# A router gate, state tables and the hand-written order of all steps rewritten in a two-layer kernel

## The reference

```python
xn = layernorm(x)                                    # layer 0
s  = complex_recurrence(xn; 32 states, A, B, C) + D * xn
g  = silu(gelu(xn @ proj1.T + b1) @ proj2.T + b2)    # hidden 1024
x  = x + s * g
xn = layernorm(x)                                    # layer 1
s  = causal_attention(xn; 16 heads, latent kv of 64, rope of 64) @ Wo
logits = xn @ router_w.T + router_b                  # 8 experts
p  = softmax(logits); keep the two largest, divide by their sum -> gate
g  = silu(xn @ base_w.T + base_b + 2 * ((xn @ lora_A) * gate) @ lora_B)
x  = x + s * g
```

## Time and profile before

| | us |
|---|---|
| median of 3 runs | 942.93 |
| lowest and highest | 942.03, 947.07 |
| the profiled execution, its own time | 945.76 |
| its span, first to last instruction | 944.0 |
| mean granted TensorE clock | 0.965 |
| busy: PE, PEld, DVE | 852.4, 770.8, 739.1 |
| busy: ACT, POOL | 544.0, 478.7 |

### The profile page before, as it was taken

The page is one execution under the profiler, slowest core; times in us unless marked ns, Lnnn a source line. Parts: engine busy times, 40 slices in busy tenths (PEclk is TensorE's granted clock), DMA queues, the critical chain, the costliest instruction groups (busy, mean ns, idle before and its releaser), DMA issues.

```text
span 944.0 us, 22803 instructions
## 1 busy us (share of the span) xinstructions
PE 852.4 (90%) x7632; PEld 770.8 (82%) x7632; DVE 739.1 (78%) x2611; ACT 544.0 (58%) x1612; POOL 478.7 (51%) x1188
## 2 busy tenths in 40 slices
PE   5778999999898589999999998999999899899986
PEld 4567998888787579798898987989889797897974
DVE  6798878988587378888888877788877888868872
ACT  4433444444545556667566675666766576665671
POOL 5722101201315466666666666576766666656661
PEclk9989999999999799999999999999999999999997
DMA  8401110000001111111111111111111111111110
GB/s 309 158 1 29 57 56 1 1 1 1 2 12 42 37 37 46 37 48 32 47 46 39 48 29 48 34 49 47 32 49 34 48 45 32 51 28 46 47 31 13
DMA packets 56278, 41.22 MB, mean 44 GB/s; under 512 B 30304, under 2 KB 53216, under 8 KB 55520
## 3 DMA queue, kind: packets, MB, share of 16 engines
q1 hardware_dynamic: 56160, 39.75, 15.3%
HBM read 14.53 MB, written 4.19 MB: 20 GB/s over the span
## 4 chain that ended last, share of the span: by engine, by line
PE 54%; DVE 23%; SPq 11%; issue 6%; POOL 4%; DMA 1%; ACT 1%; POOLq 0%; DVEq 0%; ACTq 0%
PE bank L454 32%; PE bank L640 10%; PE bank L658 7%; SPq L408 5%; SPq L420 5%; DVE SM L1424 5%; DVE PT L1444 4%; DVE qa L1411 2%; POOL par L1616 2%; POOL par L1621 1%; PE bank L516 1%; DVE st L1304 1%; PE bank L606 1%; DMA QT<-qa 1%; DVE xn L1271 1%
## 5 line engine op out<-in xcount | busy, mean ns | idle before, releaser
L1739 POOL TENSOR_SCALAR SM<-SM,stb 128x256 f32<-128x256 f32 (+1 forms) x512 | 212.2, 431 | 137.3 <-DVE stb L1432 134.7
L907 ACT ACTIVATE SM<-SM,stb 128x256 f32<-128x256 f32 (+1 forms) x512 | 226.5, 444 | 61.9 <-DVE stb L1424 60.9
L640 PE MATMUL bank<-KT,QT 128*128 128x256 f32 (+1 forms) x1024 | 206.4, 341 | 45.0 <-DVE stb L1424 33.4
L640 PEld LDWEIGHTS bank<-KT,QT 128*128 128x128 f32 x1024 | 155.1, 195 | 68.3 <-DVE stb L1424 40.1
L1424 DVE CUSTOM_DVE_ANT_0 SM<-bank,CONST 128x256 f32<-128x256 f32 (+1 forms) x512 | 155.3, 349 | 15.7 <-PE bank L640 14.3
L1444 DVE STREAM_TRANSPOSE PT<-SM 128x512 f32<-128x512 f32 x192 | 135.1, 704 | 39.2 <-PE bank L658 36.9
L454 PE MATMUL bank<-yh,wq_lo 128*128 128x256 f32 x512 | 157.2, 307 | 0.0
L454 PE MATMUL bank<-yh,wq_hi 128*128 128x256 f32 x512 | 144.3, 282 | 0.0
L454 PE MATMUL bank<-yl,wq_hi 128*128 128x256 f32 x512 | 144.2, 282 | 0.0
L795 ACT ACTIVATE hs<-bank,B 128x512 f32<-128x512 f32 x64 | 44.1, 689 | 94.5 <-PE bank L454 76.9
L454 PEld LDWEIGHTS bank<-yh,wq_lo 128*128 128x128 f32 x512 | 96.7, 189 | 1.6
(11 more groups left out here) (185 smaller groups left out, 2105.9 us busy)
## 6 DMA issues: line engine op xcount, KB each, us to landing
QT<-qa SPq DMA_DIRECT2D x512, 32.0 KB, 1.9
C<-KV SPq DMA_DIRECT2D x256, 16.0 KB, 1.8
out<-fo SPq DMA_DIRECT2D x32, 128.0 KB, 1.8
X<-in_x SPq DMA_DIRECT2D x7, 512.0 KB, 10.4
stage<-in_wqn SPq DMA_DIRECT2D x2, 1024.0 KB, 5.1
stage<-in_wo SPq DMA_DIRECT2D x2, 1024.0 KB, 5.1
stage<-in_w1t SPq DMA_DIRECT2D x4, 256.0 KB, 4.5
stage<-in_w2t SPq DMA_DIRECT2D x2, 512.0 KB, 5.6
```

What stands on the lines that cost most here:

```text
L640: i = e.matmul(sbank[n % 2][:, nk * j:nk * j + nk], Q[:, h % 8, 128 * qt:128 * qt + 128], KT[b % 3][:, h % 2, 0:nk], start=True, stop=True)
L907: i = e.activation(M[:, nk * j:nk * j + nk], M[:, nk * j:nk * j + nk], ACT.Exp, bias=S[:, 0, j:j + 1], scale=-1.0, accum_out=S[:, 1, j:j + 1])
L1739: i = e.tensor_scalar(P[:, nk * j:nk * j + nk], P[:, nk * j:nk * j + nk], S[:, 2, j:j + 1], 1.0, ALU.mult, ALU.mult)
```

## The change

It does the following.

- Gate: `e.max` gives the eight largest in order for each token tile; the third to eighth are overwritten with 3e38, `e.match_replace` puts -1e30 where the first two are found, in the logits and in a field of 3e38 at once, and one subtraction each gives two arguments for exp, whose difference is the gate. ACT's exp takes 32 columns for 16. POOL fills one field instead of the ramp (1 memset for 8). `GATE_REST` is 10 for 9.
- Tables: cosine and sine lie side by side, so one instruction does both products and sums of a doubling step (3 for 4), and the copies at the end are 5 for 10. One more piece boundary.
- POOL's parameters: the exponentials of both columns of `nuth` are made in one pass, so three passes become two; the eight multiples of the angle are issued with no wait in between. The load of `nuth` goes ahead of those of x.
- First chunks: `scan(0)` at g=9 (7), `scan(1)` and later at 12, 20, ... as before; `l0_bu(0)` at 6 (7); the outputs of chunk 1 a step later; the tables start at g=6 (3); `l0_sum` and `l0_gate` a step later for all chunks.
- Last batch: `l1_pv`, `latents` and `latents_low` for tile 0 come as soon as its units are turned (step 12 after the batch's start instead of 16), and its `l1_out` at 15 instead of 19; tile 1 follows alone.
- Passage: all eight query blocks of batch 0, and all four placements in the order 0, 3, 1, 2, come ahead of the first step; before, three placements came ahead and the fourth at step 4, behind `spread(0)`. `gate_sum(0)` comes after the four `turn_queries`.
- Other steps: `Q_AT`, `TK_AT`, `MISC_AT`, the bank order and the place of nearly every call in its step. In a batch `l1_lora` now comes first in step 9, ahead of the query block, the misc block and the turn of the keys; `mids` comes a step later on ACT; `gate_sum` comes ahead of `most`; `weigh` a step earlier.

```diff
-Q_AT = {0: (0,), 2: (1,), 5: (2, 3), 9: (5,), 10: (7, 6), 11: (4,)}
-Q0_AT = {2: (5,)}
+Q_AT = {1: (0,), 2: (1,), 5: (2, 3), 9: (7,), 10: (5,), 11: (6, 4)}
+Q0_AT = {}
-TURN_AT, TM_AT, TK_AT, LORA_AT, MISC_AT = 7, 7, 8, 9, (8, 11)
-GATE_REST = 9
+TURN_AT, TM_AT, TK_AT, LORA_AT, MISC_AT = 7, 7, 9, 9, (9, 10)
+GATE_REST = 10
...
-def summed(n, lag):
+def summed(n, lag, qt=1):
...
-    b, m = (n - lag) // UNITS, (n - lag) % UNITS
-    return b if m == UNITS - 1 and 0 <= b < NB else None
+    b, m = divmod(n - lag, UNITS)
+    last = 2 * ORDER.index(1) + 1 if b == NB - 1 and qt == 0 else UNITS - 1
+    return b if m == last and 0 <= b < NB else None
...
-            def l1_pv(b):
+            def l1_pv(b, tiles):
...
-                w.wait_ge("pt", UNITS * b + UNITS)
+                w.wait_ge("pt", UNITS * b + (UNITS if 1 in tiles else 2 * ORDER.index(1) + 2))
...
+                if 0 not in tiles:
+
+                    w.wait_ge("otl", 4 * b + 2)
...
             place(0, 0)
+            place(0, 3)
             place(0, 1)
-            place(0, 3)
+            place(0, 2)
...
             l1_q(0, 1)
-            l1_q(0, 3)
+            l1_q(0, 2)
+            l1_q(0, 0)
             free_shared("ty", 1)
             l1_turn(1, jof("ty", 1))
-            l1_q(0, 2)
             l1_q(0, 7)
+            l1_q(0, 4)
+            l1_q(0, 3)
+            l1_q(0, 5)
             l1_lora(0)
-            l1_q(0, 0)
...
-                e.activation(lg[:, 3, :, :], lg[:, 3, :, :], ACT.Exp).then_inc(SEM["gx"], 1)
+                e.activation(ex[:, :, :, :], ex[:, :, :, :], ACT.Exp).then_inc(SEM["gx"], 1)
...
-                    e.tensor_scalar(g1[:, 0:n], tsn[:, 0:n], ps, None, ALU.mult).then_inc(SEM["tab"], 1)
-                    e.tensor_scalar(g2[:, 0:n], tc[:, 0:n], ps, None, ALU.mult).then_inc(SEM["tab"], 1)
+                    n = 2 ** i
+                    e.tensor_scalar(g1[:, 0:n], tsn[:, 0:n], col(40 + i), None, ALU.mult).then_inc(SEM["tab"], 1)
+                    e.tensor_scalar(g2[:, 0:n], tc[:, 0:n], col(48 + i), None, ALU.mult).then_inc(SEM["tab"], 1)
                     took("tab", 2)
-                    e.scalar_tensor_tensor(tc[:, n:2 * n], tc[:, 0:n], pc, g1[:, 0:n], ALU.mult,
-                                           ALU.subtract).then_inc(SEM["tab"], 1)
-                    e.scalar_tensor_tensor(tsn[:, n:2 * n], tsn[:, 0:n], pc, g2[:, 0:n], ALU.mult,
+                    e.scalar_tensor_tensor(CS[:, :, n:2 * n], CS[:, :, 0:n], col(56 + i), G[:, :, 0:n], ALU.mult,
                                            ALU.add).then_inc(SEM["tab"], 1)
...
-                e.tensor_tensor(L, ML[:, :, 256:264], rb, ALU.add).then_inc(SEM["gt"], 1)
+                w.wait_ge("fill", 1)
+                e.tensor_tensor(LR[:, :, 0, :], ML[:, :, 256:264], rb, ALU.add).then_inc(SEM["gt"], 1)
                 took("gt")
-                yield from first_of(L, lv[:, 2, :], E1)
-                e.scalar_tensor_tensor(L2, E1, -3e38, L, ALU.mult, ALU.add).then_inc(SEM["gt"], 1)
+                for t in range(2):
+                    j = e.max(top[:, t, :], LR[:, t, 0, :])
+                j.then_inc(SEM["gt"], 1)
                 took("gt")
                 yield
-                yield from first_of(L2, lv[:, 3, :], E2)
-                e.tensor_tensor(E1, E1, E2, ALU.add).then_inc(SEM["gt"], 1)
-                e.tensor_tensor(L2, L, bc(lv[:, 2, :]), ALU.subtract).then_inc(SEM["gsub"], 1)
+                e.memset(top[:, :, 2:8], 3e38).then_inc(SEM["gt"], 1)
                 took("gt")
+                for t in range(2):
+                    j = e.match_replace(LR[:, t, 2:4, :], top[:, t, :], LR[:, t, 0:2, :], -BIG)
+                j.then_inc(SEM["gt"], 1)
+                took("gt")
+                yield
+                for t in range(2):
+                    j = e.tensor_scalar(ex[:, t, :, :], LR[:, t, 0:4:2, :], top[:, t, 0:1], None, ALU.subtract)
+                j.then_inc(SEM["gsub"], 1)
                 for _ in range(GATE_REST):
                     yield
...
-            exact_exp(col(1), col(3), 12, 2)
+            exact_exp(col(0, 2), col(2, 2), 2)
...
-            exact_exp(col(0), col(2), 8, 0)
             ts(col(4), col(2), 1.0, -1.0, ALU.add, ALU.mult)
-            exact_exp(col(4), mag, 8, 0)
+            exact_exp(col(4), mag, 1)
```

More of the change, by code:

```diff
@@ L108, in shared_bank_order @@
         b, m = n // UNITS, n % UNITS
+        if (d := summed(n, LAG_V, 0)) is not None:
+            if len(js) % 2:
+                js.append(("pad", len(js)))
+            js += [("v", 4 * d + i) for i in range(4)]
+        if m == TM_AT and b + 1 < NB:
+            js.append(("tm", b + 1))
         for qt in range(2):
@@ L111, in shared_bank_order @@
                 js.append(("o", 2 * d + qt))
[L112 to L118, removed]
         if m == TURN_AT and b + 2 < NB:
             js.append(("ty", b + 2))
+        if m == LORA_AT and b + 1 < NB:
+            js.append(("lo", b + 1))
         if m in MISC_AT and b + 2 < NB:
@@ L754, in _ @@
                     l1_turn(b + 2, jof("ty", b + 2))
+                if m == LORA_AT and b + 1 < NB:
+                    l1_lora(b + 1)
                 if m in MISC_AT and b + 2 < NB:
@@ L909, in exps, with latents @@
                 i.then_inc(SEM["p"], 1)
-            def latents(b):
-                w.wait_ge("pv", b + 1)
+            def latents(b, qt):
+                w.wait_ge("pv", b + 1 + (b == NB - 1 and qt))
                 if b == 0:
                     after_l0(w)
-                for i, (qt, pair) in enumerate(EVAC):
+                for pair in range(2):
+                    i = EVAC.index((qt, pair))
                     w.wait_ge("o", 2 * (b - 1) + qt + 1)
@@ L954, in _ @@
                     w1_high(3)
+                if g == 65:
+                    mids(0, wbank)
                 if g == 0:
@@ L1573, in _ @@
                             turn_queries(c + 1, u // 2)
+                go(gate, 2)
                 if 0 <= n - LAG_T < TOTAL:
@@ L1602, in _ @@
                     gate_sum(c + 1)
+                if n < TOTAL:
+                    most(n)
                 for qt in range(2):
@@ L1605, in _ @@
                         gated_out(2 * d + qt)
-                if (d := summed(n, LAG_L)) is not None:
-                    latents_low(d)
+                for qt in range(2):
+                    if (d := summed(n, LAG_L, qt)) is not None:
+                        latents_low(d, qt)
         @block.gpsimd
@@ L1821, in _ @@
             queries_sum(0, 0)
+            queries_sum(0, 3)
             queries_sum(0, 1)
-            queries_sum(0, 3)
+            queries_sum(0, 2)
             for n in range(STEPS):
                 b, m = n // UNITS, n % UNITS
+                for qt in range(2):
+                    if (d := summed(n, LAG_C[qt])) is not None:
+                        residual(2 * d + qt)
+                if m == KV_AT and b + 1 < NB:
+                    key_turn(b + 1)
+                    chain = factors(b + 2)
                 for u in Q0_AT.get(n - 2, ()):
@@ L1833, in _ @@
                             queries_sum(c + 1, u // 2)
-                if m == KV_AT and b + 1 < NB:
-                    key_turn(b + 1)
-                    chain = factors(b + 2)
-                for qt in range(2):
-                    if (d := summed(n, LAG_C[qt])) is not None:
-                        residual(2 * d + qt)
                 go(chain, 1)
```

438 lines of the change are left out of this document (212 added, 226 removed).

## The result

The changed kernel takes 903.9 us (median of 4 runs, 903.25 to 905.94), against 942.5 for the kernel before: a ratio of 0.958, 95% interval 0.955 to 0.962. Its profiled execution took 904.47 us, with a span of 902.7. The prediction's sum gave 904.9.

What follows compares the result with a forecast made beforehand. PE's work, idle waits for DVE's row maxima and lost clock were taken to bound it; periods 27, fourteenth 1.5, passage 1.5, start 5 and last batch 3 sum to 38 us, giving 904.9 us, range 888 to 928.

Steps and rivals of the forecast that it cites:

- Gate: Layer 1's gate on DVE: 2.8 us before, 1.5 after, 1.3 saved; bounds for the new gate 1.0 to 2.8.
- DVE has 15.3 us of work where PE has about 17.0, DVE no longer ends last: Period, from lora's release to the sum over keys: shorter gate and earlier lora let DVE finish before PE.
- The step on SP: Period: spreading DMAs delay group 1's placements and DVE's `turn_queries`; bound 37.3 us by SP and DVE, against PE's 36.97.
- The term of 27: Thirteen periods of layer 1: each falls from 39.78 to 37.7 us, 2.08 x 13 = 27 us gained.
- by nothing: `mids` on ACT, a step later, ends near 682.7; PE has work until 682.9 before lora, so it just fits.
- The rival by which SP holds the rest: Gate costs what it did; periods give 0.3 each by lora's place alone, other parts little: 939 us, chance 6%.
- The slower rival: ACT is behind at `mids`, PE stands at lora every period; 3.7 us of lateness gives 956 us, chance 6%.
- Passage: Layer 0 to first sum: SP's gapless queue covers the reordering; the shorter gate gives 1.5 us.
- The fourteenth period: Path through SP already the bound there, so the gate's saving comes off in full: 1.5 us.
- half of the 3.4 is lost again: Start: POOL's `skip` products, ten microseconds earlier, meet other DVE work; 1.7 us of the saving remains.
- The 1 us that the prediction worked out for that case: Start: gain of 1 instead of 5 us if POOL products each held DVE's pair instructions at the tables.
- Last batch: Tile 0's sum runs in PE's idle time, tile 1's alone takes 3.7 us; end at 941 instead of 944, -3.

Runs made afterwards that it cites:

- e8: Old gate in the changed kernel with SP's spread split in two (eight DMAs in step 5, eight in step 7): 932.14 us, ratio 0.991.
- e4: Changed kernel with SP's spread of the next batch split in two, eight DMAs in step 5 and eight in step 7: 896.67 us, ratio 0.954.
- e2: Kernel before with nothing but the new gate: 909.43 us, ratio 0.967.
- e1: Changed kernel with the old gate of fourteen dependent instructions: 942.98 us, ratio 1.002.
- e7: Changed kernel with the passage's queries, placements, turned input, lora and misc blocks in the order of before: 902.98 us, ratio 0.960.
- e3: Changed kernel with the last batch's sum over keys kept whole: 903.33 us, ratio 0.962.
- e13: Kernel before with nothing but the gate's start moved from step 1 to step 3: 924.23 us, ratio 0.980.
- e10: Changed kernel with old gate and split spread, the gate's start moved from step 1 to step 3: 921.93 us, ratio 0.979.
- e12: Changed kernel, spread whole, with nothing but the gate's start moved from step 1 to step 3: 907.15 us, ratio 0.963.
- e5: Changed kernel with POOL's two skip products of the first chunk waiting for the first Z: 904.24 us, ratio 0.961.

## Why the prediction was right, and where it was not

**The time was right, the reason for half of it was not.** 38 us were forecast; the medians give 38.6, the two profiles 41.3. By the profiles no term missed by more than 4. That the last batch and the start came near their numbers is in part luck, as shown below.

**Gate.** 1.5 us forecast for the new, 1.43 measured; 1.3 saved forecast, 1.62 measured in place (e8 against e4). By the Trainium skill, "Vector Engine (DVE) Microarchitecture Reference", on the match hardware, the replacement would be a load of values and a pass. The trace agrees (0.09 and 0.16 us), but the two pairs take 0.38 together, which is less than the 0.5 that was taken for them, so the 1.7 worked out from that rule was too long.

**Period.** The step "DVE has 15.3 us of work where PE has about 17.0, DVE no longer ends last" failed. The work is right: from lora's result at 661.53 to the end of the last turn at 678.64 there are 17.1 us, of which 1.9 are waits, so 15.2. But 1.05 of the 1.9 us of waits are for scores, which PE delivers in its own time. Work before such a wait can't be drawn on by work behind it, so a margin must be counted from the last wait that the other engine ends. From there none is left (e8). By the prediction's count the old gate with the split spread would fit, 15.2 + 1.6 = 16.8 in 17.0; it costs 2.6 us a period. The order of the periods, to which the prediction gave the release of DVE, is worth 0.1 to 0.3 (e2) or less than nothing (e1).

The step on SP was right in its place: its bound was worked out as 37.3, the period is 37.42, DVE stands where it was said, and taking the transfers out of the way gives PE's 36.95 (e4). It isn't the bound of every period, though: six of thirteen take PE's own 36.9. The term of 27 was too small by 0.3 us a period. The forecast took 39.78 less a bound, so it had the clock in it without a number of its own; in the trace it is 11.4 us of the 30.7.

**`mids`.** Forecast to fit "by nothing": it ends at 658.90, and lora starts at 658.95. PE doesn't stand there.

**Rivals.** The rival by which SP holds the rest and lora's place still gives 0.3 a period is answered by e1: with a gate as long as before the order gives -0.36, and the whole is no faster than before. The slower rival had the right kind of place (an engine a little late in each period), and 2.7 us of lateness as its point; the 1.6 us of the old gate in the new order are enough to use up all gains, as the clock goes too.

**Passage.** Right in size and in reason (e7), though SP's run without a gap goes on to 358.0, and 345.6 was only the end of the rows. The fourteenth period gained 0.6 for 1.5, and the term had no ground: no gate runs in that period. The last of the sixteen gates runs at 825 us in the changed kernel, ahead of the sum that ends the thirteenth period (829.68), and at 860 us in the kernel before (865.96). With the old gate in the changed order the fourteenth takes 34.2 (e1). SP's transfers hold DVE there for 1.80 us, and taking them away gives 33.1 (e4).

**Start.** The magnitude is ready at 34 us, as forecast. 3.9 us were found for 5, by one profile of each. The three kernels with the old layer 0 reached the first query block at 274.9, 272.1 and 272.7, and nine with the new one at 269.3 to 272.1, 270.7 in the mean: 2.6 us. The step "half of the 3.4 is lost again" was too kind: four instructions held for 1.05 us more each are 4.2 us, more than the 3.4 saved. And of the waits that the upper bound was made of 6.9 of 10.4 us went, but a new one came that no term has: PE stands 8.24 us for the first Z, where it had no such stand before. By the Trainium skill, "SBUF — State Buffer", "Who interferes with whom", an instruction with one input, `tensor_scalar`, can be held too, when it uses both of DVE's ports; L1137 (1.22 against 0.17) agrees. The 1 us that the prediction worked out for that case lies nearer to 2.6 than the 5 that was taken.

**Last batch.** Forecast 3 by the split; the split gives 1.5 (e3). Tile 1's sum alone took 5.36 us, at a granted clock of 0.68 behind a stand of 3.30, for the 3.7 worked out at full clock. The other 2.9 us of the stretch's gain come without the split: behind the start of a whole last sum e3, e2 and e13 need 17.3 to 17.7 us, the kernel before 20.3 in its profile. The granted clock over that stretch was 0.75 before and 0.89 in e3 and e2. Why it was lower there stays open; without this 2.9 the stretch would have fallen short of the 3 forecast.

## What to carry to other kernels

Where two engines feed each other, look for the last wait of the late engine that the other one ends, and count what lies between it and the next delivery: only there does an instruction's length count, and there it counts in full, with the clock that is lost on top. Halving the 2.8 us of the gate was worth 2.2 to 2.9 us a period, though DVE was busy 78% of the time. Before a step is moved out of such a stretch, look at where its second half will land: by the traces of e10 and e12 it is the gate's rest, 1.3 us or more now between the sum and `latents_low`, that took back much of what the move had won with the old gate and more than that with the new one. A queue of small DMAs can be cut: eight transfers issued two steps later took 7.2 us off the whole.

## What the runs showed of the hardware

Idle time of PE has two prices. e10 and e13 have 21.3 and 18.5 us of it in the thirteen periods, in waits of at most 0.9 us, and 482.8 and 480.2 us of busy time at a granted clock of 1.00; before, e1 and e8 have 24.4 to 27.3 us with waits up to 1.5, 2.3 and 2.1, and 489.5 to 494.6 us of busy time at 0.97 to 0.98, for the same matmuls. After the wait of 2.32 us in e1 four microseconds ran at 0.69, that is partly at 1.2 GHz instead of 2.4, and the sum over keys took 4.68 us for 4.1. So 20.0 us more of idle time cost 35.4 in e1. The same stand doesn't cost it each time: PE stands 1.8 to 2.3 us ahead of each of e1's thirteen sums, and nine of them take 4.7 to 5.8 us, four the 4.1 of full clock; in e10 to e13 all thirteen take 4.1. The runs with the longer waits also have more idle time in all, so which of the two decides isn't separated here.

A product of POOL on 512 columns holds an instruction of DVE on four or eight columns until it ends, so that it takes 1.1 to 1.2 us for 0.17, and the next instruction meets the next product: moving the products moves the loss (e5).
